# Halves of a hop summed on PE, one comparison per unit, transposed sums, and loads moved ahead of the last table

## The reference

```python
# layer 0: three hops, h0 the input
msg = (x * norm_out[:, None])[src]
agg = segment_sum(msg, dst)
x = 0.5 * (agg * norm_in[:, None]) + 0.5 * h0
# after three hops:  x @ W.T;   y = layernorm(h0 + that)
# layer 1, on y
h = relu(concat(y[src], y[dst]) @ W1 + b1)
w = sigmoid(h @ W2 + b2)
agg = segment_sum(w[:, None] * y[src], dst)
out = layernorm(y + layernorm(y + agg) * gamma + beta)
```

## Time and profile before

| | us |
|---|---|
| median of 3 runs | 1122.18 (1121.04 to 1123.58) |
| profiled execution, its own time | 1122.8 |
| its span, first to last instruction | 1121.1 |
| PE busy | 947.2 (84%), 11292 instructions |
| PE weight loads | 785.8 (70%) |
| DVE busy | 956.2 (85%), 2664 instructions |
| ACT busy | 614.6 (55%) |
| POOL busy | 496.5 (44%), 676 instructions |

### The profile page before, as it was taken

How to read it: one execution, slowest core, us unless ns; L and a number is a source line. 1 busy time by engine, 2 the same in 40 slices (tenths; PEclk the granted TensorE clock), 3 DMA queues, 4 the chain that set the end, 5 groups by cost and what they waited for, 6 DMA issues and landing times.

```text
span 1121.1 us, 33394 instructions
## 1 busy us (share of the span) xinstructions
PE 947.2 (84%) x11292; PEld 785.8 (70%) x11293; DVE 956.2 (85%) x2664; ACT 614.6 (55%) x1523; POOL 496.5 (44%) x676
## 2 busy tenths in 40 slices
PE   4889898787889888989479999999989999989950
PEld 2888888576677767777257787877767777777740
DVE  7999999589999998987479999998878888888866
ACT  6666776512100002222267777887767767767755
POOL 1000000300101003546777777777777777777711
PEclk9999999799999999999689999999989999999975
DMA  3000000000000000111476777777767776767601
GB/s 103 1 1 0 0 0 0 1 1 3 3 2 3 3 3 18 40 45 47 121 217 204 205 219 211 221 212 216 206 191 209 212 206 200 206 207 207 184 12 49
DMA packets 77517, 117.44 MB, mean 105 GB/s; under 512 B 20489, under 2 KB 38973, under 8 KB 77373
## 3 DMA queue, kind: packets, MB, share of 16 engines
q1 hardware_dynamic: 58172, 63.13, 18.8%
q0 software_dynamic: 19200, 52.45, 16.6%
HBM read 108.66 MB, written 6.86 MB: 103 GB/s over the span
## 4 chain that ended last, share of the span: by engine, by line
DVE 37%; POOL 26%; issue 16%; PE 15%; ACT 3%; DMA 1%; SPq 1%; DVEq 1%; ACTq 0%; POOLq 0%
POOL region L889 17%; POOL U L889 6%; PE bank L1772 5%; DVE stage L995 4%; DVE hx L995 3%; DVE aggT L1192 3%; DVE stage L1158 3%; DVE aggT L1167 2%; POOL stage L889 2%; DVE aggT L995 2%; DVE stage L1179 1%; DVE t L1251 1%; ACT region L2000 1%; PE bank L1869 1%; DVE t L1249 1%
## 5 line engine op out<-in xcount | busy, mean ns | idle before, releaser
L889 POOL DMA_INDIRECT region<-src_split,region x272 | 266.2, 979 | 84.8 <-issue 81.9
L1772 PE MATMUL bank<-U,region 128*128 128x256 f16 (+1 forms) x1875 | 236.8, 277 | 3.4 <-DVE U L1135 2.1
L1772 PEld LDWEIGHTS bank<-U,region 128*128 128x128 fp8e4 x1875 | 180.6, 99 | 37.3 <-DVE U L1135 2.8
L2186 ACT CAST region<-bank 128x512 f16<-128x512 f32 x338 | 180.7, 591 | 0.0
L2036 ACT CAST region<-bank 128x500 f32 x202 | 120.0, 594 | 56.0 <-PE bank L1661 46.6
L2166 ACT ACTIVATE region<-bank 128x512 f16<-128x512 f32 x169 | 100.9, 597 | 64.6 <-PE bank L1872 59.7
L1449 DVE SCALAR_TENSOR_TENSOR region<-bank,region 128x512 f16<-128x512 f32 x169 | 116.4, 688 | 15.9 <-ACT region L2166 12.4
L1869 PE MATMUL bank<-region,xs 128*128 128x256 f16 x676 | 106.0, 281 | 18.5 <-DVE region L1449 11.5
L1433 DVE TENSOR_SCALAR region<-region,stage 128x512 f16<-128x512 f16 x338 | 108.8, 363 | 9.8 <-DMA region<-slot_rows 9.8
L889 POOL DMA_INDIRECT U<-src_split,region x96 | 93.0, 969 | 29.3 <-issue 29.3
L1881 PE MATMUL bank<-U,region 128*128 128x256 f16 x676 | 105.9, 281 | 0.0
(11 more groups left out here) (293 smaller groups left out, 2320.2 us busy)
## 6 DMA issues: line engine op xcount, KB each, us to landing
region<-slot_rows SPq DMA_DIRECT2D x169, 256.0 KB
region<-in_dst_dram SPq DMA_DIRECT2D x100, 64.0 KB
region<-src_split,region POOLq DMA_INDIRECT x272
slot_rows<-aggT SPq DMA_DIRECT2D x104, 3.2 KB
src_split<-U SPq DMA_DIRECT2D x25, 64.0 KB, 1.5
src_split<-xs SPq DMA_DIRECT2D x25, 64.0 KB, 1.5
tgt_split<-q SPq DMA_DIRECT2D x25, 64.0 KB, 1.6
region<-tgt_split SPq DMA_DIRECT2D x100, 16.0 KB
```

The lines of the kernel that those rows point to most:

```text
L889: nc.gpsimd.indirect_dma_start(out=rows_of(n, i), out_offset=None, in_=src_split, in_offset=bass.IndirectOffsetOnAxis(ap=listed[n % LISTS] ...
L1772: z = nc.tensor.matmul(bank[2 * (k % 2) + p][:, 0:width], count[:, h, b * P:(b + 1) * P], U[k % 2][:, h, 0:width], start=h == 0, stop=h == ...
L2186: nc.scalar.copy(y_rows[u % 4][:, a, :], bank[3 + a][:, :]).then_inc(rows_copied, 1)
```

## The change

Eight edits, all in one kernel:

1. `hop`: two matmuls of 128 columns per source block, for the high and the low half, with the same weights and into the same columns. Hop 0's in-degree rides as the 129th column of the low half. The drains read one sum: L1270 and one of the two operations of `scaled_sums` are gone, and in hop 0 PE waits for ACT's copy (`inroot_ready`) before it reuses a bank.
2. The slot lists are stored twice, one version for each half of the partitions (`upper_targets`: the lists plus 64, made by one more ACT operation); `store_slots` issues 8 DMAs, `load_slots` 2, of 64 partitions each.
3. With them `turn_pair` is one comparison of 1024 elements.
4. `first_loads`: the first three units' lists and the first targets are loaded ahead of the last call of `tables` on SP; the waits of `fetch_pair` for the y, P and Q splits go by block; DVE's wait for all splits before the steps is gone.
5. The windows of a group are loaded in two halves, in two steps.
6. `sum_pair`: y rows as weights, weighted one-hots as moving operand, so that sums are feature-major, as 4 products of 128 and 4 of 64 columns.
7. `fold_parts`: two fp32 products; `copy_parts` copies half as much.
8. `judge_landed` before the steps, its product and flag at steps 6 and 8 (2 and 4 before), in bank 2; PE waits for the flag before the first batch sum.

```diff
@@ store_slots, load_slots, first_loads (SP)
+            def load_slots(u):
+                i, m = divmod(u, UNITS)
+                if u >= 3:
+                    sp.wait_ge(turned_ready, u - 2)
+                for h in range(2):
+                    sp.dma_start(slots_here[u % 3][h * HD:(h + 1) * HD, :],
+                                 slot_rows[i, m:m + 1, h, :].broadcast_to([HD, 8 * P])).then_inc(slots_loaded[u % 3], 16)
+
+            def first_loads():
+                sp.wait_ge(hop_psum, 3 * NB)
+                sp.wait_ge(q_tabled[FIRST_BLOCK % 2], 16 * (FIRST_BLOCK // 2 + 1))
+                sp.wait_ge(slots_stored, STORED * HALF_BLOCKS)
+                load_slots(0)
+                targets_of(0)
+                load_slots(1)
+                load_slots(2)
...
-                for a in range(2):
-                    for k in range(2):
-                        first = 64 * t + (2 * (1 - a) + k) * UNITS
-                        at = ((2 * a + k) * 2 + t) * P
-                        sp.dma_start(slot_rows[i, :, at:at + P], turned_slots[i][first:first + UNITS, :])\
+                for k in range(2):
+                    first, at = 64 * t + (2 + k) * UNITS, (2 * k + t) * P
+                    for h in range(2):
+                        sp.dma_start(slot_rows[i, :, h, at:at + P], turned_slots[i][first:first + UNITS, :])\
+                          .then_inc(slots_stored, 16)
+                    first, at = 64 * t + k * UNITS, (4 + 2 * k + t) * P
+                    for h, lists in enumerate((turned_slots[i], upper_targets[:, i, :])):
+                        sp.dma_start(slot_rows[i, :, h, at:at + P], lists[first:first + UNITS, :])\
                           .then_inc(slots_stored, 16)
...
             for c in range(NB + 2):
+                if c == NB + 1:
+                    first_loads()
                 tables(c, c % 2)
...
@@ steps (SP)
-                if s == 1:
-                    window(0, 0)
-                    window(1, 1)
-                if b is not None and b % BPS == 0 and 2 <= b // BPS + 1 < POOLED:
-                    window(b // BPS + 1, (b // BPS + 1) % 2)
+                if 2 <= s < 6:
+                    window_half((s - 2) // 2, (s - 2) // 2, s % 2)
+                if b is not None and b % BPS < 2 and 2 <= b // BPS + 1 < POOLED:
+                    window_half(b // BPS + 1, (b // BPS + 1) % 2, b % BPS)
@@ drains (DVE)
-                link(nc.vector.scalar_tensor_tensor(
-                    out=t1[p][:, :], in0=ps[:, D:2 * D], scalar=factor, in1=plus, op0=ALU.mult, op1=ALU.add))
                 nc.vector.scalar_tensor_tensor(
-                    out=t2[p][:, :], in0=ps[:, 0:D], scalar=factor, in1=t1[p][:, :], op0=ALU.mult,
+                    out=t2[p][:, :], in0=bank[2 * (k % 2) + p][:, 0:D], scalar=factor, in1=plus, op0=ALU.mult,
                     op1=ALU.add).then_inc(hop_drained, 1)
...
-                    nc.vector.tensor_tensor(t1[p][:, :], bank[p][:, 0:D], t1[p][:, :], ALU.add)\
-                      .then_inc(hop_drained, 1)
@@ turn_pair (DVE)
-                for a in range(2):
-                    z = nc.vector.tensor_scalar(turned_hot[u % 3][:, a * 4 * P:(a + 1) * 4 * P],
-                                                slots_here[u % 3][:, a * 4 * P:(a + 1) * 4 * P],
-                                                row_no[:, a:a + 1], None, ALU.is_equal)
-                z.then_inc(turned_ready, 1)
+                nc.vector.tensor_scalar(turned_hot[u % 3][:, :], slots_here[u % 3][:, :], row_no[:, 0:1], None,
+                                        ALU.is_equal).then_inc(turned_ready, 1)
@@ hop (PE)
-                    z = nc.tensor.matmul(bank[2 * (k % 2) + p][:, 0:width],
-                                         count[:, h, b * P:(b + 1) * P], U[k % 2][:, h, 0:width],
-                                         start=h == 0, stop=h == NB - 1)
+                    for half in range(2):
+                        width = D + 1 if k == 0 and half else D
+                        z = nc.tensor.matmul(bank[2 * (k % 2) + p][:, 0:width], count[:, h, b * P:(b + 1) * P],
+                                             U[k % 2][:, h, half * D:half * D + width], start=h + half == 0,
+                                             stop=h == NB - 1 and half == 1, skip_group_check=k == 0)
@@ fetch_pair (PE)
+                if at == 0:
+                    latest = max(source_block(u, 0), source_block(u, 1))
+                    pe.wait_ge(y_split, latest + 1)
+                    pe.wait_ge(pq_split, latest + 1)
                 if u % UNITS == 0:
-                    pe.wait_ge(y_split, NB)
-                    pe.wait_ge(pq_split, NB)
@@ sum_pair, fold_parts (PE)
-                        z = nc.tensor.matmul(
-                            bank[7][:, t * 2 * D:(t + 1) * 2 * D],
-                            hot_weights[u % 3][:, 2 * i:2 * i + 2, :, t].rearrange("p a r -> p (a r)"),
-                            y_rows[u % 4][:, i, t * 2 * D:(t + 1) * 2 * D],
-                            start=m + i + t == 0, stop=m == UNITS - 1 and i + t == 2, skip_group_check=True)
+                        for y_half in range(2):
+                            z = nc.tensor.matmul(
+                                bank[7][:, t * P:t * P + (2 - y_half) * HD],
+                                y_rows[u % 4][:, i, (2 * t + y_half) * D:(2 * t + y_half + 1) * D],
+                                hot_weights[u % 3][:, 2 * i:2 * i + 2 - y_half, :, t],
+                                start=m + i + t + y_half == 0, stop=m == UNITS - 1 and i + t + y_half == 3,
+                                skip_group_check=True)
...
-                for half in range(2):
-                    for a in range(2):
-                        z = nc.tensor.matmul(bank[2][:, P:2 * P], fold[:, (1 - half) * HD:(1 - half) * HD + P],
-                                             att_parts[:, (2 * half + a) * D:(2 * half + a + 1) * D],
-                                             start=half + a == 0, stop=half + a == 2)
+                for part in range(2):
+                    z = nc.tensor.matmul(bank[2][:, P:2 * P], att_parts[:, part, :, :].rearrange("p t r -> p (t r)"), ident[:, :],
+                                         start=part == 0, stop=part == 1)
@@ copy_lists (ACT)
+                nc.scalar.activation(upper_targets[64 * t:64 * t + BUCKETS, i, :], here[0:BUCKETS, 0:P], ACT.Identity,
+                                     bias=half_offset[0:BUCKETS, 0:1])
```

More of the change, by code:

```diff
@@ L285, in gnn_kernel @@
         earlier = carve(stage, taken, [P], f16)
-        att_parts = carve(stage, taken, [4 * D])
-        fold = carve(stage, taken, [3 * HD])
-        row_no = carve(stage, taken, [2])
+        att_parts = carve(stage, taken, [2, 2, HD])
+        fold = carve(stage, taken, [P])
+        row_no = carve(stage, taken, [1])
         units = carve(stage, taken, [2], f16)
@@ L670, in _, with window_half @@
                 sp.wait_ge(q_tabled[p], 16 * ((NB + 1 - p) // 2))
-            sp.wait_ge(hop_psum, 3 * NB)
-            def window(n, p):
-                if n >= 2:
-                    sp.wait_ge(ohT_ready, n - 1)
-                    sp.wait_ge(s_psum, (n - 1) * BPS)
-                first = load_four(ET.SP, base[0], n, N)
-                for q in range(BPS):
-                    sp.dma_start(qwin[p][q * QR:(q + 1) * QR, :], tgt_split[bass.ds(first[q], QR), :])\
+            window_first = [None]
+            def window_half(n, p, half):
+                if half == 0:
+                    if n >= 2:
+                        sp.wait_ge(ohT_ready, n - 1)
+                        sp.wait_ge(s_psum, (n - 1) * BPS)
+                    window_first[0] = load_four(ET.SP, base[0], n, N)
+                for q in range(half * BPS // 2, (half + 1) * BPS // 2):
+                    sp.dma_start(qwin[p][q * QR:(q + 1) * QR, :], tgt_split[bass.ds(window_first[0][q], QR), :])\
                       .then_inc(win_loaded[p], 16)
-                for q in range(BPS):
                     at = n * (BPS * BE) + q * BE
@@ L1839, in sums @@
                 pe.wait_ge(ohw_ready, b + 1)
+                if b == 0:
+                    pe.wait_ge(flag_ready, 1)
                 if b:
@@ L1918, in _ @@
                 if 0 <= u - 3 < TOTAL:
-                    if u == 3:
-                        pe.wait_ge(flag_ready, 1)
                     sum_pair(u - 3)
@@ L1927, in _ @@
                     sums((b - 3) // BPS, (b - 3) % BPS, blocks_folded(s - 1))
-                if s == 2:
+                if s == 6:
                     pe.wait_ge(chain["verdict"], 7)
-                    nc.tensor.matmul(bank[7][0:1, 0:3], one[:, :], verdict_sums[:, :], start=True, stop=True)\
+                    nc.tensor.matmul(bank[2][0:1, 0:3], one[:, :], verdict_sums[:, :], start=True, stop=True)\
                       .then_inc(verdict_psum, 1)
@@ L2057, in first_sums @@
                     hold(act, b)
[L2058 to L2060 removed]
```

(13 more changed lines are left out.)

84 lines of the change are left out of this document (34 added, 50 removed).

## The result

| | before | changed |
|---|---|---|
| median of 4 runs each, same chip | 1122.88 us (1121.04 to 1123.63) | 1115.47 us (1114.97 to 1118.88) |
| ratio, 95% interval | | 0.9951 (0.9931 to 0.9970) |
| the same, second session | 1121.62 us | 1116.38 us, 0.9956 (0.9940 to 0.9972) |
| profiled execution, its own time and span | 1122.8, 1121.1 | 1118.9, 1117.1 |
| first to last gather started | 549.05 to 1062.44 us | 542.65 to 1059.20 us |

By the ratios the kernel is faster by 5.5 and 4.9 us (by the medians of the two sessions 7.4 and 5.2); 14.7 were forecast. The profiled execution is 3.4 us over its median; a second profile of the same kernel (`after_again`) has a span of 1114.3 us; its gathers have the same mean within 2 ns and start at 541.80.

The account below looks back on a forecast made before the run. POOL's 400 gathers were taken to bound the attention stage, DVE and PE alternately the hops. From 1122.8 us, 13.6 for the hops, 0.3 net for the gathers' start and 0.8 for the tail gave 1108.1 us, range 1099 to 1121.

Parts of the forecast that it names:

- POOL's waits for PE: Attention stage: POOL's three waits for PE, 2.9 us in all, would be gone because PE starts earlier.
- What bounds the kernel, and the hops: POOL's 400 gathers bound the attention stage; in the hops, shorter drains less dearer products save 13.6 us.
- rival A: Hop products: the second weight load is not hidden, a half costs 99 ns, kernel slower at 1250 us; chance 0.07.
- Comparison, sums, fold: Attention stage and tail: one comparison saves at most 0.1 us, sums' PE savings lie under POOL; tail gives -0.8 us.
- Rival D: Last stage grows: gathers start 4.8 us late and each costs 10 ns more under queue traffic, 1114 us; chance 0.10.
- Lists ahead of the last table: Before the attention stage: eight DMAs on SP delay the last table and the gathers by 2.6 us, bounds zero and 4.8.
- Storing the lists twice: In the hops: doubled list DMAs and an extra ACT operation cost nothing; without cover up to 5 us.
- B: Hops: PE takes over at once, shorter drains only lengthen DVE's idle time, gain 2 us or less, about 1120.7; chance 0.13.
- C: Hops: shorter drains also untangle the engines, DVE's whole removed time comes off, 23.5 us, 1099 us; chance 0.14.

Follow-up runs that it names:

- hops_alone: Kernel before with only the hop change (two halves of 128 columns, drains reading one sum): 1109.28 us, ratio 0.9884.
- hops_sums: Kernel before with the hop change, feature-major sums and the fold of two products, all else as before: 1107.86 us, ratio 0.9875.
- two_compares: Changed kernel with first loads behind the last table and each unit's comparison in two instructions of 512 elements: 1107.64 us, ratio 0.9865.
- changed_two: Changed kernel with only the comparison of a unit in two instructions of 512 elements again: 1111.48 us, ratio 0.9905.
- lean: lean_pool_zero with the clear of aggT moved from POOL to DVE, behind the judge: 1104.27 us, ratio 0.9849.
- one_list: Changed kernel with first loads behind the last table and each unit's list loaded by one transfer instead of two: 1644.26 us, ratio 1.4645.
- lean_pool_zero: two_compares with each slot list stored once (4 transfers per half block) and loaded by one transfer, clear still on POOL: 1105.44 us, ratio 0.9850.
- two_compares_2: two_compares run again unchanged, in a later session: 1107.27 us, ratio 0.9864.
- extra_sbuf: two_compares with an added DVE comparison of 1024 elements in a row ahead of every second unit, result unread: 1112.94 us, ratio 0.9926.
- extra_strided: two_compares with an added DVE comparison of 512 elements two apart ahead of every second unit, result unread: 1114.06 us, ratio 0.9942.
- four_compares: two_compares with each unit's comparison in four instructions of 256 elements: 1109.79 us, ratio 0.9900.

## Why the prediction was wrong

| part | forecast | measured |
|---|---|---|
| hops (edit 1) | -13.6 | -13.0 (hops_alone) |
| sums and fold (6, 7) | -0.8 | -1.0 (hops_sums less hops_alone) |
| lists twice, windows, judge, first loads behind the table, with POOL's waits for PE (edits 2, 5, 8, rest of 4) | -2.9 and 0 | -1.1 (two_compares less hops_sums) |
| first loads ahead of the last table | +2.6 | +4.5 (changed_two less two_compares) |
| one comparison of 1024 | 0 | +5.2 to +5.7 (changed less changed_two) |
| sum | -14.7 | -5.4 to -4.9; the kernel itself -4.9 and -5.5 |

The rows are steps between neighbouring kernels, from the kernel before to the changed one, so that their sum meets the kernel by construction and proves nothing. Each step is uncertain by some 2 us or more: -1.0 and -1.1 cannot be told from nothing, the others can. Of the 9.3 to 9.8 us between forecast and measurement, 5.2 to 5.7 are the comparison, 1.9 the lists' place, 1.8 the third row and 0.6 the hops.

*What bounds the kernel, and the hops: right.* The pair of halves costs 115 ns (57.4 each), and rival A is gone. The 81 ns of the Trainium skill, page "TensorE: Matmul & The Clock Gate", section "Back-to-back issue gap", which the prediction quotes, is not seen: 57.4 ns over 99 steps. Between the first products of each hop and the last of all, hops_alone has 102.2, 91.7 and 117.2 us for 103.5, 97.7 and 121.4: -1.3, -6.0 and -4.2, where 4.4, 6.1 and 3.1 stood. Hop 1 went as worked out, with PE late next, and has 91.7 us in all 16 profiles with edit 1. Hop 0 has 99.3 to 102.2 us in them and hop 2 117.1 to 118.7, with the same hop code, so that single profiles size those two terms to 1.5 to 3 us only. Two small steps of the working do not come out of the rows: 0.13 x 5.5 is 0.7, not 0.6, with no row for the 5.5, and PE's part on the path is 2.0, not 2.1. Neither matters.

*The failed step: "Comparison, sums, fold".* "A single one saves at most one start, 0.1 us", it says, and it priced one comparison for two as DVE time, "all of it under POOL", which was right for the time and wrong for the gathers. The 0.13 us that DVE saves per unit pay nothing, and with one instruction of 0.49 us in place of two of 0.36 each of 400 gathers takes 13 ns more in the mean, 5.2 us, on the one engine that bounds the stage. The argument that POOL is the bound was in the first paragraph; the price of a gather was then taken as fixed. Rival D, with 0.10, had the gathers 4.8 us late and "each of 400 costs 10 ns more" for queue traffic, 1114 us: both sizes came near, but the cause of the second was another (two_compares, which has the same transfers, takes it away).

*Lists ahead of the last table: mechanism right, term too small.* SP took 5.1 us from the first of the eight to the table's store for 4.3 reckoned, and started them when POOL's clear began (534.79 and 534.95), not 1.6 us before: block 24's p was stored 4.95 us after the start of the clear, where it had been 0.09. Two things were mis-sized. Six halves took 3.67 us on SP (1.15 and 2.52) where 3.0 stood: a half costs SP as much as a full list. And block 23's rows came later against the clear (533.67 for 534.95, before 543.71 for 546.10), because POOL, after its wait of 2.67 us for a q buffer, split blocks 23 and 24 one behind the other. The landing, 2.75 us, was as worked out (2.8). The start came 4.75 us later; 4.8 was the bound above. PE's early start bought little if anything: with the loads ahead POOL waited for PE 0.3 to 0.9 us, with them behind 0 to 2.6 (0.3 in lean; one_list apart).

*Storing the lists twice* was costed at nothing. POOL's waits for a q buffer at the end of hop 2 were 2.67 us (1.05 before). Over all profiles they sum to 0.9 to 3.0 us with the doubled stores and to 0 to 1.7 without. By lean_pool_zero against two_compares (0.9850 for 0.9865) the price may be 1.7 us, second loads included; the intervals overlap.

*POOL's waits for PE* fell by 2.0 us, to 0.9, where none were forecast. Whether fewer waits mean more gathers held up is not shown: changed_two's gathers work 390.7 us, as before, hops_alone's 388.5.

*Rivals:* B falls (hops_alone), C too (13.0, not 23.5).

## What to carry to other kernels

Where POOL's gathers bound a stage, price each DVE instruction between SBUF tiles by how long it can hold a gather up, not by DVE's time. Here two short ones beat one long one, and four were no better than two. Transfers that are moved ahead of another on a queue cost their whole issue time to whoever waits for that other; move them only if the engine that sets the pace needs them. A saving on an engine off the critical path is worth nothing, but its side effects on the engine that bounds are worth their full price.

## What the runs showed of the hardware that was not expected

- A gather of 128 rows, 0.95 us when undisturbed, that starts while DVE is inside an instruction between SBUF tiles lasts longer by that instruction's remaining time less 0.13 us (0.22 and 0.09 us in the rows above; 81 gathers of the changed kernel to within 0.01 us). Where the gather is first, DVE is held instead: of the changed kernel's long comparisons, the 26 that began 0.4 to 0.7 us after a gather lasted 0.58 us in the mean and up to 0.72, where the median of all is 0.48.
- A broadcast load of 128 partitions whose source has an outermost dimension of two (one_list) is slow, 46 to 50 GB/s. DVE's comparisons there, one per list of 256 KB, and DVE's waits for lists (us in total, times, longest):

```profile
902.38 0.48 DVE L1434 TENSOR_SCALAR region<-region,stage 128x1024 f16<-128x1024 f16 x1 [2.60 <-DMA region<-slot_rows]
908.09 0.49 DVE L1434 TENSOR_SCALAR region<-region,stage 128x1024 f16<-128x1024 f16 x1 [3.81 <-DMA region<-slot_rows]
913.25 0.49 DVE L1434 TENSOR_SCALAR region<-region,stage 128x1024 f16<-128x1024 f16 x1 [2.39 <-DMA region<-slot_rows]
```

```profile
DVE region L1434 <- DMA region<-slot_rows: 568.5, 158, 11.3
```

  One list comes per 5.2 to 5.7 us, where the same bytes as one row for 128 partitions, or as two transfers of 64, let a unit pass in under 3 us. By the Trainium skill, page "DMA: Bandwidth & Descriptors", section "Why a DMA increments its semaphore by 16 and not by 1", the slowest dimension (of a size over 1) of a transfer's two sides decides over how many of 16 DMA engines it is spread: the largest number up to 16 that divides both, here two. The trace agrees in time; it does not show the engines one by one.
- Kernels with the same code up to there began their gathers between 534.9 and 538.0 us (two_compares, two_compares_2, extra_sbuf, extra_strided, four_compares): a difference under 3 us between two single profiles says nothing on where the stage begins.
